# VectorE moves a turned probability block two steps back instead of three, in a two-layer attention kernel

## The reference, cut to what matters

```
q = [q_nope (32), rope(q_rope) (64)]
a1 = softmax(causal(q k1^T / sqrt(96))) v1      # k1, v1 from a 32-wide latent, shared rotary key
a2 = softmax(q ks^T / sqrt(96)) vs              # 32 selected tokens, no mask
a3 = softmax(causal(q kw^T / sqrt(96))) vw      # k, v straight from x
out = gate0 * a1 + gate1 * a2 + gate2 * a3 ;  out @ w_proj
```

## Time and profile before

| | us |
|---|---|
| median of 3 runs | 2321.69 |
| lowest, highest | 2316.57, 2322.24 |
| the profiled execution's own time | 2312.3 |
| its span, first to last instruction | 2310.5 |
| TensorE matmul busy in it | 1911.7 |
| VectorE, ScalarE busy | 1367.5, 1163.8 |
| mean granted TensorE clock (share of full) | 0.90 |

### The profile page before, as it was taken

How to read it: one execution, slowest core, us unless ns; L and a number is a source line. 1 busy time by engine, 2 the same in 40 slices (tenths; PEclk the granted TensorE clock), 3 DMA queues, 4 the chain that set the end, 5 groups by cost and what they waited for, 6 DMA issues and landing times.

```text
span 2310.5 us, 40290 instructions
## 1 busy us (share of the span) xinstructions
PE 1911.7 (83%) x10620; PEld 1069.9 (46%) x10620; DVE 1367.5 (59%) x4228; ACT 1163.8 (50%) x3476; POOL 645.1 (28%) x659
## 2 busy tenths in 40 slices
PE   3433357999899998999899989999899899989985
PEld 2221224555445544555455545555455455545542
DVE  5999833656555555555555555555565655565563
ACT  1112213656556565556465655565565556556651
POOL 0323233323323332323232322323232323332200
PEclk7556556999999998989998999899998999899998
DMA  3000002111101110111111111111111111111101
GB/s 137 0 0 0 0 14 53 44 41 36 51 19 40 35 50 23 36 32 40 36 34 36 42 43 33 33 46 42 34 33 45 42 34 33 35 52 31 35 1 37
DMA packets 71349, 81.44 MB, mean 35 GB/s; under 512 B 29521, under 2 KB 37842, under 8 KB 70994
## 3 DMA queue, kind: packets, MB, share of 16 engines
q1 hardware_dynamic: 71122, 78.74, 13.2%
HBM read 7.90 MB, written 2.10 MB: 4 GB/s over the span
## 4 chain that ended last, share of the span: by engine, by line
PE 69%; DVE 17%; issue 8%; ACT 3%; DVEq 1%; POOL 1%; SPq 1%; DMA 0%; ACTq 0%; POOLq 0%
PE bank L1652 21%; PE bank L1672 14%; PE bank L1612 9%; DVE arena L1349 4%; PE bank L1522 4%; PE bank L1523 4%; DVE arena L1341 3%; PE bank L1623 2%; PE bank L1564 2%; PE bank L1545 2%; PE bank L1518 1%; PE bank L1577 1%; PE bank L1560 1%; DVE arena L1106 1%; PE bank L1585 1%
## 5 line engine op out<-in xcount | busy, mean ns | idle before, releaser
L1341 DVE CUSTOM_DVE_ANT_0 arena<-bank,W 128x512 f32<-128x512 f32 (+3 forms) x1024 | 502.0, 490 | 711.4 <-PE bank L1652 573.4
L1652 PE MATMUL bank<-arena 96*128 96x512 f32 (+6 forms) x2048 | 785.6, 466 | 30.8 <-issue 18.3
L903 ACT ACTIVATE arena<-arena 128x512 f32<-128x512 f32 (+3 forms) x1024 | 572.8, 559 | 442.5 <-DVE arena L1341 439.2
L1672 PE MATMUL bank<-W,arena 128*128 128x128 f32 x2560 | 487.1, 288 | 97.1 <-DVE arena L1349 92.0
L1672 PEld LDWEIGHTS bank<-W,arena 128*128 128x128 f32 x2560 | 306.2, 142 | 464.3 <-DVE arena L1349 226.0
L1652 PEld LDWEIGHTS bank<-arena 96*128 96x128 f32 x2048 | 341.1, 199 | 174.6 <-issue 149.7
L1349 DVE COPY arena<-bank 128x512 f32<-128x512 f32 (+2 forms) x768 | 356.2, 464 | 2.0 <-issue 1.5
L685 POOL TENSOR_TENSOR arena<-arena,one 128x512 f32<-128x512 f32 x64 | 66.7, 1042 | 950.6 <-DVE arena L1311 939.7
L1612 PE MATMUL bank<-arena 128*32 128x256 f32 (+1 forms) x3072 | 227.6, 369 | 8.3 <-DVE arena L1349 7.7
L903 ACT ACTIVATION_READ_ACCUMULATOR arena<-arena 128x1 f32 x1024 | 194.8, 190 | 0.0
L886 ACT ACTIVATE arena<-bank 128x384 f32<-128x384 f32 x256 | 125.6, 491 | 116.2 <-PE bank L1672 116.0
(11 more groups left out here) (260 smaller groups left out, 2259.3 us busy)
## 6 DMA issues: line engine op xcount, KB each, us to landing
arena<-arena SPq DMA_DIRECT2D x896, 64.0 KB, 2.0
arena<-arena SPq DMA_DIRECT2D x64, 128.0 KB, 2.4
W<-wide SPq DMA_DIRECT2D x1, 3730.0 KB, 13.3
X<-x SPq DMA_DIRECT2D x8, 256.0 KB, 5.5
out<-arena SPq DMA_DIRECT2D x8, 256.0 KB, 2.2
arena<-arena SPq DMA_DIRECT2D x96, 16.0 KB, 1.9
LW<-lat SPq DMA_DIRECT2D x1, 768.5 KB, 14.3
arena<-mods SPq DMA_DIRECT2D x1, 768.0 KB, 4.5
```

The source lines that it names most:

```text
L903: A(Pb[:, s % 4, 0:n], Pb[:, s % 4, 0:n], ACT.Exp, bias=nmax[:, s:s + 1], scale=-1.0, accum_out=lsum[:, c:c + 1]).then_inc(s_p, 1)
L1341: v.tensor_tensor_reduce(Pb[:, s % 4, 0:n], bank[turn.score_bank(s)][:, lo:lo + n], w("mask", T - n), -1.0, 3e38, ALU.add, ALU.min, nmax[: ...
L1652: MM(bank[turn.score_bank(s)][:, 0:lo + n], query(t), Kb[a][0:QD, g % 2, h, skip:skip + lo + n], start=True, stop=True).then_inc(s_qk, 1)
L1672: last = pe.transpose(bank[3 + k % 2][:, c * P:(c + 1) * P], Pb[:, k % 4, c * P:(c + 1) * P], ident)
```

## The change

One constant: VectorE moves the turned block of unit s - 2 behind the row maximum of unit s, instead of that of unit s - 3. ScalarE's moves, the transposes and every wait's value stay as they are; the steps at which VectorE's moves stand shift one earlier in its list.

```diff
--- before.py
+++ after.py
@@ -60,7 +60,7 @@
 GU = len(units(1))
 GR = 2
 RU = GU // GR
-T_LAG, D_LAG = 2, 3
+T_LAG, D_LAG = 2, 2
 PV_TALL, PV_LOW = 11, 19
 INVERT, SPREAD, MOVE, NORM, ADD = 16, 19, 21, 23, 24
 MOVER = {3: "dve", 2: "act", 1: "dve", 0: "dve"}
```

## The result

The changed kernel took 2178.2 us (median of 4 runs, 2165.71 to 2182.94) against 2321.97 us before (4 runs): a ratio of 0.938 with a 95% interval of 0.934 to 0.942, 144 us less. A second set of six runs, beside the experiments, gave 2176.4 us and 0.940 (0.936 to 0.944). The forecast was 2199 us, 123 us less.

The account below looks back on a forecast made before the run. TensorE was taken as the attention's bound, held most by VectorE's moves: 99.7 us idle time plus 37 us restarts, 137 us gross, less 9.5 and 4.4 us, gives 123 us; 2321.7 - 123 = 2199 us, range 2165 to 2264.

Parts of the forecast that it names:

- The mechanism: Attention: transposes wait for a VectorE move queued behind another unit's row maximum; 99.7 us idle, products with V included, would go.
- The next wait: Transposes, mostly unit 9 in group 2's second half, would wait on exponentials (L903) instead, 10 to 20 us in all.
- The norm's exception: Group 0, unit 15: removing the 0.31 us wait gains nothing, as the norm (L1252) starts no earlier; 0.63 us per turn, 4.4 us.
- The cover of the moves: Tall steps: the move, waiting for its own transposes, hides behind the next scores; lateness added was taken as nothing.
- one of the signs that I had named against my sum: Fillings of bank 7 showing new waits on their reader would mean that the forecast sum is wrong.
- part of it comes back: Rival, chance 0.21: bank 7 fillings and weight loads wait instead, half the gain is lost, about 60 us remain; 2262 us.
- What each of these waits really costs: Attention's 208 removed waits: each costs 0.18 us more than its idle time, 37 us in all.
- the exception of 9.5 us: Group 2's second half: unit 9's transposes still come late behind VectorE's picks; 1.35 us not gained, 7 times.
- The clock's rival: Rival, chance 0.16: shorter stops keep the clock up in group 2's second half in four later batches; 29 us more, 2170 us.
- the working that I gave the larger chance: The main sum for the whole kernel: 123 us gained, 2199 us, chance 0.55, own range 2180 to 2235 us.

Follow-up runs that it names:

- e1: Against the kernel before: lag kept at three, but VectorE's move of unit s - 3 goes ahead of the row maximum of unit s; 2190.9 us, ratio 0.943.
- e2: Against the kernel before: lag 2 for VectorE's moves of t = 3 alone, t = 1 and t = 0 stay at lag 3; 2240.6 us, ratio 0.966.
- e3: Against the kernel before: lag 2 for VectorE's moves of t = 1 and t = 0 alone, t = 3 stays at lag 3; 2262.0 us, ratio 0.974.
- e7: Against the changed kernel: VectorE's move of unit 2 of every row alone goes back to lag 3; 2207.9 us against 2176.4 us.
- e9: Against the changed kernel: group 0's next norm is made ahead of the move and the inverses at step 16; 2161.8 us, ratio 0.932 to the kernel before.
- e4: Against the changed kernel: lag 2 kept, but the move of unit s - 2 goes ahead of the row maximum of unit s; 2278.2 us, ratio 0.982 to before.
- e0: The changed kernel run again unaltered, beside the experiments; 2176.4 us, ratio 0.940 to the kernel before.
- e8: Against e9: group 2's four one-hot picks of 32 columns made as one comparison of 128 columns; 2136.9 us, ratio 0.921 to the kernel before.

## Why the prediction was right, point by point

**The mechanism** was right. The transposes of unit k waited for the move of unit k - 2 behind the maximum of unit k - 1, and for nothing else: 92.0 us became nothing that the waits view shows. e1 shows the "behind a maximum" half of it, e2 and e3 that the waits of the two halves are independent of each other, and e7 puts one of them back.

**The next wait** was named with its place and size. I forecast 10 to 20 us on L903, mostly at unit 9 of group 2's second half, some 1.7 us a time; measured 11.0 us, 9 cases, the longest 1.5 us. The stretch gained 1.8 us at full clock (forecast: 0.43 for unit 4 and 0.7 to 1.6 for unit 8).

**The norm's exception** held too. The 0.31 us wait before it brought nothing and L1473's wait grew, from 2.15 us a turn to

```profile
1284.11 0.63 PE L1473 MATMUL bank<-W,arena 128*128 128x128 f32 x4 [2.82 <-DVE arena L1252]
```

that is by 0.67 us (forecast 0.63). e9 shows that this norm stood needlessly behind the move. What I left out was the clock: the whole stretch was longer than before by 1.2 us in the windows shown.

**The cover of the moves** was there for the transposes: no lateness of the exponentials but at the places named, and two waits of 0.3 us at the end. e4 shows what it looks like where it is missing. But one of the signs that I had named against my sum did appear, a filling of bank 7 that waits for its reader: L1522 on L828, 7.6 us in 14 new waits. That is the rival "part of it comes back", at 7.6 us where it had about 60, and my sum had it at nothing. VectorE's busy time, forecast the same, is 1385.1 against 1367.5 us; its instructions, added one by one, take 1602 us in both, so its records overlap less and the work is the same.

**"What each of these waits really costs"**, 0.18 us beside the idle time, or 37 us, was right on the average. In the 40 rows that ran at the full clock in both profiles, the changed kernel gains 96.6 us where 147 waits with 67.4 us of idle time stood: 0.20 us each beside the idle time. It is no constant. The second halves of groups 1 and 3, where the 4.2 us above were gained for 5 waits with 2.7 us, give 0.31 us each; the first halves of groups 0 and 2 next to nothing, and there the new waits of L1522 stand. e7's 0.57 us, 0.3 us over the idle time, is a mean over both levels of the clock and can't be put on all 208 waits: at the full clock e2 and e3 have 0.2 us over it in both halves.

**Where the 21 us come from** by which the gain of 144 us is above the forecast one. Between the two profiled spans it is 129 us, and 140 us with e0's profile, whose span is 2170.5 us. Sums over the eight second halves of group 2, and over those of group 0, in the three profiles:

| | before | after | e0 |
|---|---|---|---|
| group 2's second halves, us | 288.0 | 260.8 | 242.7 |
| group 0's second halves, us | 268.4 | 274.3 | 279.6 |

In group 2's second halves the forecast has 18 waits with 19.7 us of idle time and the exception of 9.5 us, a gain of 13.5 us. It was 27 and 45 us. In those of group 0 it has 5 us; there 6 and 11 us were lost. All the other rows but the last give 104.6 and 103.7 us, where the forecast has 100. So the terms of the waits hold to about 5 us, and what the forecast missed lies in two stretches, with opposite signs, and in both of them the clock moved (below). The rest of the distance is which execution is taken. The kernel before was profiled in a fast one, 2312.3 us where the median is 2322, the changed one in its slowest. At the same mean clock of 0.900 single runs took 2312.3 and 2315.1 us before and 2178.7 and 2179.0 us after, 133 to 136 us less.

**The clock's rival** came true in part, beside the working that I gave the larger chance. The mean granted clock in group 2's second half, in the seven batches that have the picks:

| | |
|---|---|
| before | 1.00, 0.92, 0.79, 0.82, 0.79, 0.79, 0.82 |
| after | 1.00, 1.00, 1.00, 0.81, 0.83, 0.81, 0.82 |
| e0, the same kernel | 1.00, 1.00, 1.00, 1.00, 1.00, 1.00, 0.83 |
| e9 | 1.00, 0.81, 1.00, 0.81, 1.00, 0.81, 1.00 |
| e8 | 0.91, 0.91, 0.91, 1.00, 1.00, 0.94, 1.00 |

The stop in this stretch is 2.27 us before, 1.5 us in the next three rows of the table and gone in e8. So a median of 2178 us inside the range of 2165 to 2264 is part skill and part luck: the waits were priced rightly, and two effects of the clock that the main working left out, a gain in group 2's second halves and a loss in group 0's, partly cancel. In the execution profiled for e0 the clock stayed up in the batch where it fell above:

```profile
1167.05:1197.93 30.88, 27.89 (x197) 18.24 (x195) 22.19 (x71) 18.34 (x65) 7.31 (x7) 1.00 0.13 33
```

The two profiles of one kernel are 10.6 us apart, and this one stretch is 5.9 us of it. So with the stop of 1.5 us, whether the clock falls there is a matter of the execution, which fits the width of the runs, 2166 to 2197 us over both sets. The Trainium skill ("TensorE: Matmul & The Clock Gate", section "HAM oscillation - how this bites in real kernels") names stops of TensorE as what brings it down. The rows agree in group 0's second half: with a wait on the norm of 2.15 us before, 2.82 us in the changed kernel and 1.12 us in e9, the mean clock in the batch shown is 0.91, 0.87 and 0.97. In group 2's second half they agree only in part: in e8, where the stop is gone, the clock is still below full in four of seven batches, though less far. The mean clock of whole runs is highest in e8, 0.908 to 0.914 against 0.903 to 0.907 in e9 and 0.895 to 0.906 in the changed kernel. No run here changed a stop and nothing else.

## What to carry to other kernels

In a software pipeline, ask of each instruction in an in-order list what it waits for and what it could already do: an evacuation whose data has long been there belongs ahead of, or a step away from, an instruction that waits for fresh data, while an evacuation whose data is not yet there must not stand ahead of one that could run (the first was worth 128 us in e1, the second cost 100 us in e4). Price a removed wait above its idle time where the waiting engine is the bound; here a wait of 0.25 us cost 0.39 to 0.6 us at the full clock. And compare stretches at an equal clock before a gain is put down to a term. And when several small operations stand in the stretch that is then critical, make them fewer rather than move them.

## What the runs showed of the hardware that I had not expected

A short stop of TensorE costs more than the idle time that the profile gives it, about 0.2 us more: 0.17 us on the average of e7's 38 waits at the full clock (0.14 and 0.33 us in the two rows shown), 0.20 us on that of the 147 waits that the change removed there.

Four comparisons of 32 columns with a pointer scalar took 2.42 us on VectorE, 0.6 us each, and one comparison of 128 columns with broadcast operands took 0.84 us.

At the back edge of the loop TensorE stands still with no semaphore to explain it: 2.7 to 3.5 us in each of six turns before, 2.4 to 4.0 us in the changed kernel, 3.4 to 4.3 us in e0, the same kernel once more. The wait before, over the whole span, and then one such place in each kernel:

```profile
PE bank L1652 <- issue: 18.3, 7, 3.5
```
```profile
1316.00 1.22 PE L1652 MATMUL bank<-arena 96*128 96x512 f32 x1 [4.03 <-issue]
```
```profile
1382.11 1.22 PE L1652 MATMUL bank<-arena 96*128 96x512 f32 x1 [2.99 <-issue]
```

Of the two places the first is the changed kernel's, the second the same one before, 1.0 us shorter. This is the largest difference of the six; at the last of them the changed kernel's stop is 0.4 us shorter. The Trainium skill ("Runtime: NRT & Kernel Launch", section "Instruction fetch mechanics") says that a taken branch to a page that is not at hand has to wait for a fetch by DMA. No run here tells this apart from other causes, and the stop differs as much between executions of one kernel as between the two; its cause stays open.
